# First attention's setup: what is computed ahead of the first batch, and in which order

## What is computed

```
x = x + attention0(layernorm(x), ctx)      # 16 batches, 64 context rows each
x = x + expert_choice(layernorm(x))        # every expert picks its tokens
x = x + attention1(layernorm(x), ctx, masks)
x = x + zone_mixture(layernorm(x))         # 8 experts, weights per token
```

## Time and profile before

| | |
|---|---|
| profiled execution, its own time | 2457.34 us |
| its span | 2455.3 us |
| PE busy, whole span | 2240.3 us (91%) |
| DVE busy, whole span | 1461.8 us (60%) |
| ACT busy, whole span | 861.8 us (35%) |
| POOL busy, whole span | 374.3 us (15%) |
| chain that ended last | PE L143, L144, L145: 14% each; DVE 2%; issue 1% |

### The profile page before, as it was taken

How to read it: one execution, slowest core, us unless ns; L and a number is a source line. 1 busy time by engine, 2 the same in 40 slices (tenths; PEclk the granted TensorE clock), 3 DMA queues, 4 the chain that set the end, 5 groups by cost and what they waited for, 6 DMA issues and landing times. The chain is left out here.

```text
span 2455.3 us, 40334 instructions
## 1 busy us (share of the span) xinstructions
PE 2240.3 (91%) x15302; PEld 1932.5 (79%) x15303; DVE 1461.8 (60%) x3147; ACT 861.8 (35%) x1210; POOL 374.3 (15%) x352
## 2 busy tenths in 40 slices
PE   7999998536999958999998699999999999999998
PEld 4888887325988856787787588888888888888887
DVE  6787876583445436777776584554544545545544
ACT  2455554122454413454443432222222222222222
POOL 3111110204557540111110410000000000000000
PEclk9999999755999979999999799999999999999999
DMA  2121211203435331111111400000000000000000
GB/s 73 53 68 60 77 60 47 61 0 102 74 71 105 57 52 35 52 68 60 60 52 52 144 28 27 27 3 25 26 26 26 26 26 26 26 26 26 26 9 9
DMA packets 110137, 115.05 MB, mean 47 GB/s; under 512 B 16080, under 2 KB 98768, under 8 KB 110032
## 3 DMA queue, kind: packets, MB, share of 16 engines
q1 hardware_dynamic: 97744, 96.49, 12.4%
q0 software_dynamic: 12288, 17.05, 4.2%
HBM read 62.92 MB, written 50.59 MB: 46 GB/s over the span
## 5 line engine op out<-in xcount | busy, mean ns | idle before, releaser
L1857 DVE TENSOR_TENSOR zmix_hid<-zmix_act_gate,psum 128x1024 f32<-128x1024 f32 x128 | 156.3, 1221 | 372.0 <-issue 346.7
L143 PE MATMUL psum<-zmix_wd_hi,zmix_hid_hi 128*128 128x256 f32 x1024 | 289.5, 283 | 2.3 <-DVE zmix_acc L1848 2.3
L145 PE MATMUL psum<-zmix_wd_hi,zmix_hid_lo 128*128 128x256 f32 x1024 | 289.8, 283 | 0.0
L144 PE MATMUL psum<-zmix_wd_lo,zmix_hid_hi 128*128 128x256 f32 x1024 | 289.7, 283 | 0.0
L1808 ACT ACTIVATE zmix_hid_hi<-zmix_hid 128x1024 fp32r<-128x1024 f32 x128 | 135.5, 1059 | 395.2 <-PE psum L145 276.7
L1800 ACT ACTIVATE zmix_act_gate<-psum 128x1024 f32<-128x1024 f32 x128 | 131.6, 1028 | 378.0 <-PE psum L145 378.0
L604 PE MATMUL psum<-att_v_cur,att_probs 128*128 128x96 f32 x2048 | 252.7, 278 | 4.5 <-ACT att_probs L732 3.1
L604 PEld LDWEIGHTS psum<-att_v_cur,att_probs 128*128 128x128 f32 x2048 | 240.8, 193 | 14.5 <-ACT att_probs L732 4.0
L1862 DVE TENSOR_TENSOR zmix_hid_lo<-zmix_hid,zmix_hid_hi 128x1024 fp32r<-128x1024 f32 x128 | 157.8, 1232 | 135.2 <-ACT zmix_hid_hi L1808 134.3
L1848 DVE SCALAR_TENSOR_TENSOR zmix_acc<-psum,zmix_weight,zmix_acc 128x256 f32<-128x256 f32 x512 | 211.7, 475 | 1.6 <-PE psum L145 1.6
L143 PE MATMUL psum<-zmix_xT_hi,zmix_wg_hi 128*128 128x512 f32 x512 | 201.9, 394 | 11.2 <-DVE zmix_xT_lo L1837 11.2
(11 more groups left out here) (288 smaller groups left out, 4534.1 us busy)
## 6 DMA issues: line engine op xcount, KB each, us to landing
x<-att_x_new SPq DMA_DIRECT2D x32, 512.0 KB, 2.9
att_x_in<-in_x SPq DMA_DIRECT2D x16, 512.0 KB, 3.8
rows<-att_normed_new SPq DMA_DIRECT2D x16, 512.0 KB, 3.0
att_x_in<-x SPq DMA_DIRECT2D x16, 512.0 KB, 3.9
turned<-att_newT SPq DMA_DIRECT2D x16, 512.0 KB, 2.8
zmix_xn<-turned SPq DMA_DIRECT2D x16, 512.0 KB, 4.4
zmix_acc<-x SPq DMA_DIRECT2D x16, 512.0 KB, 4.2
out_x<-zmix_acc SPq DMA_DIRECT2D x16, 512.0 KB, 3.2
```

The costliest lines, as they stand in the source:

```text
L143: pe.matmul(out, st_hi, mv_hi, start=first, stop=False)
L144: pe.matmul(out, st_hi, mv_lo, start=False, stop=False)
L145: return pe.matmul(out, st_lo, mv_hi, start=False, stop=last)
L1857: dve.tensor_tensor(hid[:, :, :], act_gate[:, :, :], psum[:, 2:4, :], ALU.mult).then_inc(up_out, 1)
```

## The change

What it does: `high_parts` splits Wq and Wo ahead of the keys' high parts. The low part of Wq becomes a helper of its own (`query_weights`), which DVE does ahead of the keys' low parts; Wo's low part (`rest`) goes behind `input_lo(0)`. PE goes from the turned rows of batch 0 straight to its queries, then makes values 0 to 3, and the maxima run without values between. Values 4 to 9 are made in body 0 between the two halves of the scores, values 10 to 15 behind the queries of batch 1; PE then waits for all values to be copied ahead of the first weighted values. In DVE's body 0, `ahead_of_new` (low parts of batch 1's rows) comes ahead of the layernorm, with values 4 to 9 between them; values 10 to 15 follow `between` (batch 1's `queries_lo`). That order of body 0 holds for the second attention too, without values. POOL copies batch 0's values when four are there, and waits for all 16 ahead of its work for batch 1.

```diff
     def high_parts(act):
+        act.wait_ge(qo_loaded, 32)
+        act.activation(kv["wq_hi"][:, :, :], wq[:, :, :], ACT.Copy).then_inc(split_hi, 1)
+        act.activation(kv["wo_hi"][:, :, :], wo[:, :, :], ACT.Copy).then_inc(split_hi, 1)
         act.wait_ge(small_loaded, 5 * 16)
         for m in range(KC):
             for n in range(2):
...
-        act.wait_ge(qo_loaded, 32)
-        act.activation(kv["wq_hi"][:, :, :], wq[:, :, :], ACT.Copy).then_inc(split_hi, 1)
-        act.activation(kv["wo_hi"][:, :, :], wo[:, :, :], ACT.Copy).then_inc(split_hi, 1)
...
+    def query_weights(dve):
+        dve.wait_ge(split_hi, 1)
+        dve.wait_ge(qo_loaded, 32)
+        dve.tensor_tensor(kv["wq_lo"][:, :, :], wq[:, :, :], kv["wq_hi"][:, :, :].bitcast(F32), ALU.subtract).then_inc(split_lo, 1)
+
     def rest(dve):
         dve.wait_ge(split_hi, 2)
-        dve.wait_ge(qo_loaded, 32)
-        dve.tensor_tensor(kv["wq_lo"][:, :, :], wq[:, :, :], kv["wq_hi"][:, :, :].bitcast(F32), ALU.subtract).then_inc(split_lo, 1)
         dve.tensor_tensor(kv["wo_lo"][:, :, :], wo[:, :, :], kv["wo_hi"][:, :, :].bitcast(F32), ALU.subtract).then_inc(split_lo, 1)
...
+        VALUES_FIRST, VALUES_HALF = 4, 10
...
             def input_side(b, p, half):
                 at_start = isinstance(b, int) and b == 0
+                if setup and isinstance(b, int) and b == 1:
+                    pool.wait_ge(setup["v_out"], 2 * B)
...
             if setup:
-                pool.wait_ge(setup["v_out"], 2 * B)
+                pool.wait_ge(setup["v_out"], 2 * VALUES_FIRST)
                 own_values(0, 0)
...
                 if there(b - 1):
                     outputs(b - 1)
+                elif setup:
+                    for n in range(VALUES_FIRST, VALUES_HALF):
+                        setup["values"](pe, n)
                 scores(b, p, 1)
                 if nxt:
                     queries(b + 1, 1 - p)
+                if setup and not there(b - 1):
+                    for n in range(VALUES_HALF, B):
+                        setup["values"](pe, n)
+                    pe.wait_ge(setup["v_out"], 2 * B)
...
                 turn_input(0, 0)
-                for b in range(0, 4):
-                    setup["values"](pe, b)
                 pe.wait_ge(setup["split_lo"], 1)
                 queries(0, 0)
-                for b in range(4, 8):
+                for b in range(0, VALUES_FIRST):
                     setup["values"](pe, b)
-                maxima(0, 0, 0)
-                for b in range(8, 12):
-                    setup["values"](pe, b)
-                maxima(0, 0, 1)
-                for b in range(12, B):
-                    setup["values"](pe, b)
+                for c in range(KC):
+                    maxima(0, 0, c)
...
                 else:
+                    ahead_of_new()
+                    if setup:
+                        for n in range(VALUES_FIRST, VALUES_HALF):
+                            setup["values_out"](dve, n)
                     layernorms(b, p, half)
-                    ahead_of_new()
                     between()
+                    if setup:
+                        for n in range(VALUES_HALF, B):
+                            setup["values_out"](dve, n)
...
             if setup:
                 setup["context_twice"](dve)
+                setup["query_weights"](dve)
                 for i in range(2 * KC):
                     setup["keys_out"](dve, i)
-                setup["rest"](dve)
             input_lo(0)
             if setup:
-                for b in range(0, 4):
-                    setup["values_out"](dve, b)
+                setup["rest"](dve)
             input_norm(1, 1, col=TT)
             queries_lo(0, 0)
+            if setup:
+                for b in range(0, VALUES_FIRST):
+                    setup["values_out"](dve, b)
             dve.wait_ge(cleared, 2)
             for c in range(KC):
-                if setup:
-                    for b in range(4 + 4 * c, 8 + 4 * c):
-                        setup["values_out"](dve, b)
                 maxima(0, c, range(TT))
-            if setup:
-                for b in range(12, B):
-                    setup["values_out"](dve, b)
             maxima_copy(0)
...
             dve.tensor_copy(limits[:, :], cand[:, :].bitcast(F32).to_broadcast([P, P])).then_inc(found_all, 1)
+            setup["query_weights"](dve)
             setup["rest"](dve)
```

More of the change, by code:

```diff
@@ L345, in setup_parts @@
     return dict(load=load, clear=clear, turn_context=turn_context, keys=keys, values=values, context_out=context_out,
-                           high_parts=high_parts, context_twice=context_twice, keys_out=keys_out, rest=rest, values_out=values_out, turned_twice=turned_twice, v_out=v_out,
+                           high_parts=high_parts, context_twice=context_twice, keys_out=keys_out, query_weights=query_weights, rest=rest, values_out=values_out, turned_twice=turned_twice, v_out=v_out,
                            k_out=k_out, split_lo=split_lo, small_loaded=small_loaded)
```

## The result

| | before | after |
|---|---|---|
| median of 20 runs each | 2454.15 us (2449.94 to 2458.41) | 2459.01 us (2454.95 to 2462.76) |
| ratio, 95% interval | | 1.0019 [1.0012, 1.0027] |
| profiled execution, its span | 2457.34, 2455.3 us | 2459.33, 2457.3 us |
| first scores of batch 0 | 49.88 | 39.93 |
| first weighted values | 61.32 | 62.37 |

By the 0.3% bound this is no change, as forecast (2458.8, the sum +1.7). The interval leaves out 1 all the same: a small slowdown is there. Against the execution that the sum was made on, the changed kernel's took 2.0 us more. Against the medians it is 4.9 us, more than twice as much: there the prediction missed something, and most experiments went after it.

The account below looks back on a forecast made before the run. PE, busy for 91% of the span, was taken as the bound, with gains only where it waits. -9.7 + 11.3 + 0.1 = +1.7 on the profiled 2457.34 gives 2459.0, in medians 2458.8 us; range 2452.0 to 2464.5.

Parts of the forecast that it names:

- Ahead of the scores: Setup up to batch 0's scores: they start at 40.2 instead of 49.88 us, -9.7.
- The stall behind POOL: Setup on DVE: Wo's low part waits for POOL's L512; without it all 2.0 us sooner, bounds 0 and 2.35.
- rival A: Setup: the lock does not hold Wo's low part, all 2.0 us sooner, 2456.8; 0.22 together with TensorE keeping 2.4 GHz.
- TensorE at 1.2 GHz at the maxima: Batch 0's maxima: TensorE at 1.2 GHz, 2.0 us from transpose to scores; at 2.4 GHz 0.4 less.
- Body 0: First attention, scores to weighted values, now with 12 of 16 values: 22.8 us instead of 11.44, +11.3.
- Rival B: Body 0: the moved values are truly hidden, it costs 2 us more only; 2449.4, faster by 0.31%; chance 0.06.
- Rival C: TensorE stays at 1.2 GHz from the maxima through the first weighted values; 2467, slower by 0.4%; chance 0.10.
- The added waits: POOL's wait for all 16 values holds back its batch 1 work and the load of batch 3: costs nothing, just hidden.
- Second attention and choice: DVE's first reciprocal in the second attention later, between 0 and +1.5, taken as +0.1; splits in choice of tokens 0.
- The sum: Whole kernel, made at the first weighted values: -9.7 + 11.3 + 0.1 = +1.7 on the profiled 2457.34, so 2459.0 us.
- the carry from the profiled execution to the medians: Whole kernel: the profiled time lies 0.3 above the median of 2457.08, so 2459.0 becomes 2458.8 in medians.

Follow-up runs that it names:

- layernorm in the gap: Changed kernel with batch 2's layernorm in DVE's idle time of body 0, all twelve values behind it, values 10 to 15 ahead of batch 1's queries: 2454.38 us, ratio 1.0000.
- the run without the stall: Changed kernel with POOL's residual rows of batch 0 held until DVE has done batch 1's normed rows: 2456.06 us, ratio 1.0009.
- filled: Changed kernel with ten unused products on PE behind each half of batch 0's maxima, where it idled: 2455.67 us, ratio 1.0007.
- version with four values: Changed kernel with values 4 to 15 left out on PE and DVE, their parts of the result zero: 2443.15 us, ratio 0.9952.
- the transposes: 22 unused transposes on PE ahead of the context's: in the kernel before 2452.16 us, ratio 0.9995; in the changed kernel 2458.20 us, ratio 1.0019.

## Why the prediction was right, and where it was not

- **Ahead of the scores** (-9.7): -9.95, scores at 39.93 for 40.2. Split, low parts and queries came within 0.3 us.
- **The stall behind POOL** (2.0 of it): sized right, but charged to the path, and in this execution to the wrong operation. Wo's low part took 0.68, and L827 took the whole stall, 3.47 - 1.38 = 2.1; with layernorm in the gap Wo's low part took it, so which of the two stands changes with a small shift, as rival A says. But the second high part of the queries ends at 26.68 + 0.69 = 27.4, so without the stall the low queries end at 28.1 instead of 28.8: 0.7 at most was on the path, and in the run without the stall nothing was. Rival A's 2.0 us were not there to be had. By the Trainium skill (SBUF — State Buffer, "SBUF: two separate sides") a DVE operation in a 2-port mode, or with two SBUF inputs while the GpSimd instruction reads SBUF, is blocked by a GpSimd instruction that started first, to its end; the trace agrees, with 3.47 against 1.37 for the same four.
- **TensorE at 1.2 GHz at the maxima**: right (0.50 in 36 to 46, 1.96 us from the transpose to the scores for the 2.0 of the earlier trace rows), and worth the 0.4 given for it (1.50 when filled).
- **Body 0** (+11.3): +11.0, 22.44 for 22.8. Low parts 46.25 for 46.4, values 4 to 9 out at 51.3 for 51.5, low queries 57.3 for 57.8, last value 62.3 for 62.9. The 0.4 is the layernorm, 4.5 for 4.9. Rival B fell, as DVE and PE took turns over the values. Rival C did not come: behind waits of 1.37 and 0.70 the values kept the full rate.
- **The added waits** (nothing): right, by 0.3 us. POOL's second copy starts at 62.48, and masked keys are there at 64.03, when PE asks at 64.32.
- **Second attention and choice** (+0.1): the first reciprocal +0.75, a batch on 0. The splits in the choice found ACT idle.
- **The sum** (+1.7 on the profiled execution): +1.05 at the weighted values, +2.0 in the span. The first is the test of the sum; that the second is as near is luck. 1.7 us came back in the last body of the first attention, where TensorE's clock fell before (0.84 in 412 to 422) and not after (1.00 in 413 to 423). 3.8 were lost in the choice of tokens, where PE waits for the first gathered rows, before and after:
```profile
592.50 1.94 PE L1345 MATMUL psum<-main_ident,moe_rows 128*128 128x128 f32 x8 [16.46 <-DMA moe_rows<-rows,moe_idx_get]
```
```profile
596.04 1.94 PE L1355 MATMUL psum<-main_ident,moe_rows 128*128 128x128 f32 x8 [20.25 <-DMA moe_rows<-rows,moe_idx_get]
```
This wait was 16.3 to 16.5 us in twelve of the fourteen profiles, four versions of the changed kernel with the values moved among them, and 20.2 in two (the changed kernel, and its version with four values). So the 3.8 us are not the change's; why the wait has two lengths is open. From there to the end 1.5 came back.

- **What failed: the carry from the profiled execution to the medians.** I took 0.3 off and called it done. The median of the three shown runs, 2457.08, lies 2.9 above that of twenty, 2454.15, and the sum fell 3.2 short of the difference of the medians: that 2458.8 met 2459.01 is the luck of two errors of one size. The profile was of a late start. Against an early one the change costs 62.56 - 57.76 = 4.8 at the mark: 2.7 as the queries go ahead of values 0 to 3, which leaves PE without work until DVE's low parts are there and the values for later, and 2.1 for the moved values. If the 46 of 117 runs in before's lower group are the early starts, 0.4 x 4.8 + 0.6 x 1.05 = 2.6 of the 4.9 us follow from this; that they are is not shown.
- **Open: the other 2 us, and whether the start alone makes the groups.** With the transposes before's median fell by 1.3 us only, and those times (2449.20 to 2456.30) are no single group, though two of twelve lie above 2453.9 where 17 of 35 of before do. The profiled execution with four values in the changed kernel had the early start and was the slowest of its four, by 6.8 us. The rest behind the mark scattered from 2388.6 to 2397.8 over executions that run the same instructions there, more than the 3.6 between the two starts: the stretch from the last turned maxima of the first attention to the first of the second took 526.9 to 533.1, the one from there to the end 1520.9 to 1524.3. So a rival for the groups, something behind the first attention such as the wait of two lengths, stands untested. The medians of the unchanged kernel, 2456.11 and 2453.68, differ by 2.4 us. So the sign of the slowdown stands better than its size: the five medians of before lie at 2453.4 to 2456.1, those of the changed kernel, alone and with the transposes, at 2459.0 and 2458.2.

## What to carry to other kernels

Ahead of adding a sum to a median, look whether the run times shown lie in groups, and of which kind the profiled execution is: here the start, with TensorE's clock low for longer or shorter, had two lengths, and at the mark the change cost 1 us for one and 5 for the other. When a sum and a profile agree, compare them at the mark for which the sum was made: in the span, 3.8 us from a wait that has nothing to do with the change made the agreement look good. Work that fills one wait (values 0 to 3, ahead of DVE's low parts) leaves that wait empty when it is moved. And work put into the next stretch's waits gains only what the second engine in the alternation (DVE, copying each value) leaves free; count its idle time, not PE's. Below 0.2% time the unchanged kernel a second time under another name, and believe the difference only beyond that.

## What the chip showed that I had not expected

- The 16 key products took 7.13 us or 9.0 to 9.7 in executions of like programs, and the record of the granted clock rises to 1.00 by 10.4 us in the first and from 14.6 us on in the others. The Trainium skill (TensorE: Matmul & The Clock Gate, "Part 1: The HAM clock gate") says that the number of slow products at a kernel's start changes from run to run, that it costs under 1% and that one should not fit to it; the traces agree with the first two, but the 3.6 us of 2455 between the two starts (61.32 and 57.76) are as large as what was to be measured here.
- Over the 97 runs of before that were timed beside the experiments, the mean granted clock goes with the time: 2450.6 us on average at 0.957 (7 runs), 2451.0 at 0.956 (24), 2454.5 at 0.955 (50), 2457.0 at 0.954 (15), 2461.1 at 0.953 (1). That it causes the difference is not shown.
- Keeping TensorE busy with unused products held the clock here but only moved the fall: 2.4 GHz at the maxima (0.97), then 1.2 GHz at the first values behind the next wait, of 2.05 us.
- PE's wait for the first gathered rows in the choice of tokens has two lengths, 16.3 to 16.5 us (twelve profiles) and 20.2 (two).
